# A two-layer vision tower on one core: layer 1 runs twelve attention tiles ahead of layer 2 instead of eight

## The reference, cut to what matters

```python
h = patches(x) @ W.T                                   # 3136 tokens x 192
h = layernorm(h + attn1(h))                            # 12 heads of 16, 49 tokens each
# layer 2
probs   = softmax(h @ Wg.T + bg); top_w, top_idx = top_k(probs, 2)
hw      = (h @ A + ba) * combine[:, :, None]           # 8 experts x rank 16
qkv     = h @ Wqkv.T + bqkv + 2 * (hw @ Bm + combine @ bb)
h = layernorm(h + softmax(q k^T / 4) v @ Wproj.T + bproj)
```

## Time and profile before

| | |
|---|---|
| median of 3 runs | 392.89 us (392.25 to 393.26) |
| the profiled execution, its time | 392.47 us |
| its span, first to last instruction | 390.7 us |
| mean granted clock of TensorE | 0.998 |
| busy: TensorE matmuls, weight loads, VectorE, ScalarE, GpSimd | 373.3, 327.3, 301.5, 218.5, 124.6 us |
| first transpose of probabilities (start of slot 1), of tile 63 (end of slot 63) | 24.58 us, 380.93 us |

### The profile page before, as it was taken

The page is one execution under the profiler, slowest core; times in us unless marked ns, Lnnn a source line. Parts: engine busy times, 40 slices in busy tenths (PEclk is TensorE's granted clock), DMA queues, the critical chain, the costliest instruction groups (busy, mean ns, idle before and its releaser), DMA issues.

```text
span 390.7 us, 13738 instructions
## 1 busy us (share of the span) xinstructions
PE 373.3 (96%) x5312; PEld 327.3 (84%) x5312; DVE 301.5 (77%) x814; ACT 218.5 (56%) x692; POOL 124.6 (32%) x262
## 2 busy tenths in 40 slices
PE   5999999999999999999999999999999999989984
PEld 4888788988888898988889889888888978878973
DVE  7367777687777788987878888787798888698872
ACT  1344646564646645566655566655664565664642
POOL 1312422321433424133315233341325241423313
PEclk9999999999999999999999999999999999999999
DMA  8732522121131122210123201111011101110111
GB/s 269 232 99 62 137 55 54 36 55 48 20 110 24 26 39 73 81 59 9 18 66 70 66 8 29 17 31 22 21 17 29 29 21 19 18 33 14 25 36 37
DMA packets 49338, 20.68 MB, mean 53 GB/s; under 512 B 41262, under 2 KB 45713, under 8 KB 49274
## 3 DMA queue, kind: packets, MB, share of 16 engines
q1 hardware_dynamic: 45530, 10.43, 12.7%
q10 hardware_dynamic: 3744, 9.38, 7.6%
HBM read 12.57 MB, written 2.41 MB: 38 GB/s over the span
## 4 chain that ended last, share of the span: by engine, by line
PE 86%; DVE 5%; ACT 3%; issue 2%; DMA 2%; POOL 1%; SPq 0%; POOLq 0%; ACTq 0%
PE ps L494 12%; PE ps L572 9%; PE ps L599 9%; PE ps L610 7%; PE ps L584 6%; PE ps L621 5%; PE ps L544 4%; PE ps L548 4%; PE ps L546 4%; PE ps L622 4%; PE ps L524 3%; PE ps L530 2%; PE ps L528 2%; PE ps L566 2%; PE ps L642 2%; PE ps L632 2%
## 5 line engine op out<-in xcount | busy, mean ns | idle before, releaser
L965 DVE TENSOR_REDUCE psum<-probs 113x12 f32<-113x588 f32 x64 | 48.6, 760 | 33.9 <-ACT probs L808 33.9
L822 ACT COPY pt<-ps 113x339 f32<-113x339 f32 x128 | 50.2, 445 | 33.4 <-PE ps L599 32.8
L939 DVE TENSOR_REDUCE mx<-ps 113x12 f32<-113x588 f32 x64 | 48.7, 761 | 17.1 <-PE ps L572 16.6
L494 PE MATMUL ps<-tokw,xs 128*128 128x192 f32 (+1 forms) x300 | 56.3, 336 | 4.4 <-DMA tokw<-in_tokw 4.1
L443 POOL TENSOR_SCALAR shift<-mv,rstd 128x1 f32<-128x1 f32 (+1 forms) x50 | 14.2, 283 | 141.6 <-ACT rstd L857 141.6
L432 POOL TENSOR_SCALAR kbd<-k,const 64x294 f32<-64x294 f32 x64 | 34.7, 552 | 73.2 <-ACT q L801 67.5
L494 PEld LDWEIGHTS ps<-tokw,xs 128*128 128x128 f32 (+1 forms) x300 | 48.9, 192 | 7.1 <-DMA xs<-in_x 4.7
L599 PE MATMUL ps<-const,probs 113*113 113x113 f32 x384 | 50.0, 266 | 4.6 <-DVE probs L974 4.0
L599 PEld LDWEIGHTS ps<-const,probs 113*113 113x113 f32 x384 | 44.3, 178 | 9.5 <-issue 8.0
L974 DVE TENSOR_TENSOR probs<-probs,rsum 113x588 f32<-113x588 f32 x64 | 50.1, 782 | 2.2
L946 DVE TENSOR_TENSOR probs<-ps,mx 113x588 f32<-113x588 f32 x64 | 49.4, 772 | 2.2
(11 more groups left out here) (93 smaller groups left out, 785.0 us busy)
## 6 DMA issues: line engine op xcount, KB each, us to landing
xs<-in_x ACTq DMA_DIRECT2D x22, 384.0 KB, 3.8
vbd<-vrow SPq DMA_DIRECT2D x160, 18.4 KB
out<-o SPq DMA_DIRECT2D x24, 96.0 KB, 1.8
xs<-in_x SPq DMA_DIRECT2D x2, 384.0 KB, 6.4
tokw<-in_tokw ACTq DMA_DIRECT2D x3, 192.0 KB, 3.6
w<-in_w SPq DMA_DIRECT2D x1, 472.5 KB, 4.2
xs<-in_x SPq DMA_DIRECT2D x3, 128.0 KB, 3.4
add<-in_add SPq DMA_DIRECT2D x1, 361.5 KB, 7.2
```

The source lines that it names most:

```text
L494: last = nc.tensor.matmul(ps[0:k, bank, 0:E], xs[:, b % XS, m, 0:k], tokw[:, m, :], start=(m == 0), stop=(m == KX - 1))
L822: nc.scalar.copy(pt[n % 2][:, 3 * half:3 * half + 3, :].rearrange("p g i -> p (g i)"), ps[0:PP, 2 + half, 0:3 * PP]).then_inc(pt_ready[hal ...
L939: nc.vector.tensor_reduce(mx[n % 2][:].rearrange("p (b h) -> p b h", b=2), score_view(n), AX.X, ALU.max).then_inc(mx_ready, 1)
L965: nc.vector.tensor_reduce(psum[:].rearrange("p (b h) -> p b h", b=2), probs_view(n), AX.X, ALU.add).then_inc(sum_ready, 1)
```

## The change

`LEAD` goes from 8 to 12, and the planner's slots follow from it. Worked through with 12, the arithmetic gives the plan below. "qk+v 22" is `project_qk2` and `project_v` of block 22, "L1 9" `project_qkv1` of block 9, "emb" an embedding, "t1" `transpose_h1` and `route`, "hw" `transpose_hw`, "out" an output projection counted in the slot by the timing above.

| slot | before | after |
|---|---|---|
| 6 | t1 2, qk+v 0, hw, out | t1 2, emb 8, hw, out |
| 7 | L1 7, emb 8, hw, out | L1 7, emb 9, hw, out |
| 8 | t1 3, qk+v 1, out | t1 3, L1 8, out |
| 9 | t1 4, emb 9, hw | t1 4, L1 9, emb 10, hw |
| 10 | t1 5, qk+v 2, hw | t1 5, qk+v 0, hw, out |
| 13 | L1 9, out | t1 7, L1 11, emb 12, hw |
| 25 | emb 16 | L1 15, out |
| 26 | t1 11, qk+v 8, hw, out | L1 16, emb 17, hw, out |
| 52 | t1 21, qk+v 18, hw | t1 22, out |
| 53 | L1 24, out | qk+v 18, hw, out |
| 54 | qk+v 19, hw, out | t1 23, qk+v 19, out |
| 55 | qk+v 20, out | t1 24, qk+v 20, hw, out |
| 56 | t1 22, out | qk+v 21, hw, out |
| 57 | qk+v 21, hw, out | qk+v 22, out |
| 58 | t1 23, out | qk+v 23 |
| 59 | t1 24, qk+v 22 (urgent), hw, out | out |
| 60 | qk+v 23, hw, out | qk 24 (urgent), out |
| 61 | qk+v 24 (urgent) | nothing but its tile |
| 62 | out | v 24, out |
| 63 | out | out |

Slots with only a layer 1 projection and no output projection are 17, 43 and 51 before, 47 after. Slots with only an embedding are 25 and 33 before, 21, 29 and 37 after. Slots in which `transpose_h1` uses bank 6 are 4 and 5 before, 4, 5, 8, 9 and 13 after. The slots of the after plan that are neither in the table nor named here repeat kinds of the before plan, up to a `transpose_h` more.

Three more edits go with it. The values of the last block are projected in slot 62, after the scores of tile 63, into bank 7, and `keep_busy` and the scores of tile 63 wait accordingly. `inverse_deviation` of layer 1 goes ahead of `take_y` in a slot n when slot n+1 has a `transpose_h1` and no output projection (with a norm to do in slots 9, 13, 21, 29, 37, 47 and 53 of the after plan). `h1_bank` gets a branch for bank 5 in slots with an urgent block; the only such slot of the after plan is 60, which has no `transpose_h1`, so the branch is never taken.

```diff
--- before.py
+++ after.py
@@ -29,7 +29,7 @@
 HB2 = 8
 AW = NB + S - 1
 RING = 6 * T
-LEAD = 8
+LEAD = 12
 XS = 5
 OS = 3
 VR = 6
@@ -152,6 +152,8 @@
 
 def h1_bank(n):
 
+    if any(urgent(b) for b in qkv2s(n)):
+        return 5
     return 6 if turns(n) and not qkv2s(n) else 4
 
 
@@ -555,7 +557,7 @@
                     if n == LAST:
 
                         pe.wait_ge(L2.qk_ready, BLOCKS)
-                        pe.wait_ge(L2.v_rows, BLOCKS)
+                        pe.wait_ge(L2.v_rows, BLOCKS - 1)
                     else:
                         pe.wait_ge(sub_ready, n)
                 else:
@@ -576,12 +578,12 @@
                                 start=(L is L2), stop=(L is L2 or m == 2))
                 last.then_inc(scores_done, 1)
 
-            def project_v(L, b, parts, free):
+            def project_v(L, b, parts, free, bank=5):
                 k = tokens(b)
                 if free:
                     pe.wait_ge(*free)
                 for m, (src, w) in enumerate(parts):
-                    last = nc.tensor.matmul(ps[0:k, 5, 0:E], src[:, 0:k], w[:, V0:V0 + E],
+                    last = nc.tensor.matmul(ps[0:k, bank, 0:E], src[:, 0:k], w[:, V0:V0 + E],
                                             start=(m == 0), stop=(m == len(parts) - 1))
                 last.then_inc(L.v_done, 1)
                 return L.v_rows, b + 1
@@ -658,7 +660,7 @@
 
             def keep_busy(count):
 
-                pe.wait_ge(hw_ready, BLOCKS)
+                pe.wait_ge(L2.v_rows, BLOCKS)
                 for _ in range(count):
                     nc.tensor.matmul(ps[:, 7, 0:128], ident, ident, start=True, stop=True)
 
@@ -701,9 +703,13 @@
                         keep_busy(3)
                     if n == LAST - 1:
                         scores(L2, attention(LAST)[1], LAST)
+
+                        project_v(L2, BLOCKS - 1, values2(BLOCKS - 1), (hw_ready, BLOCKS), 7)
                 for b in turns1(n):
                     if h1_bank(n) == 6:
                         bank6 = transpose_h1(b, 6, bank6)
+                    elif h1_bank(n) == 5:
+                        bank5 = transpose_h1(b, 5, bank5)
                     else:
                         bank4 = transpose_h1(b, 4, bank4)
                 for b in qkv2s(n):
@@ -713,7 +719,8 @@
                         pe.wait_ge(b2_loaded, 16)
                     if urgent(b):
                         bank4 = project_qk2(b, bank4)
-                    bank5 = project_v(L2, b, values2(b), bank5)
+                    if b < BLOCKS - 1:
+                        bank5 = project_v(L2, b, values2(b), bank5)
                     if not urgent(b):
                         bank4 = project_qk2(b, bank4)
                 for b in turns(n):
@@ -807,12 +814,12 @@
                 p = probs[n % 2][:, :, 0:S]
                 nc.scalar.activation(p, p, ACT.Exp).then_inc(exp_ready, 1)
 
-            def take_v(L, b, at, slot_of):
+            def take_v(L, b, at, slot_of, bank=5):
                 k = tokens(b)
                 act.wait_ge(L.v_done, b + 1)
                 if b >= VR:
                     act.wait_ge(pv_done, slot_of[last_tile(b - VR)] + 1)
-                nc.scalar.copy(L.vrow[b % VR][0:k], ps[0:k, 5, at:at + E]).then_inc(L.v_rows, 1)
+                nc.scalar.copy(L.vrow[b % VR][0:k], ps[0:k, bank, at:at + E]).then_inc(L.v_rows, 1)
 
             def take_pt(n):
                 if n >= 2:
@@ -883,13 +890,20 @@
                     take_k2(b)
                     if turns(n) or embeds(n) or urgent(b):
                         take_q2(b)
-                    if urgent(b):
+                    if urgent(b) and b < BLOCKS - 1:
                         take_v(L2, b, 0, SLOT2)
                 for b in turns(n):
                     take_v(L1, b, NB, SLOT1)
                 if not (n <= 1 and turns(n)):
                     for b in embeds(n):
                         take_h(b, embed_bank(n))
+                if n == LAST - 1:
+                    take_v(L2, BLOCKS - 1, 0, SLOT2, 7)
+
+                norm_first = bool(turns1(n + 1) and not out1(n + 1) and not out2(n + 1))
+                if norm_first:
+                    for b in out1(n):
+                        inverse_deviation(L1, b)
                 if before:
                     take_y(n - 1, u)
                 if n == LAST - 1:
@@ -899,8 +913,9 @@
                     for b in qkv2s(n):
                         if not urgent(b):
                             take_q2(b)
-                for b in out1(n):
-                    inverse_deviation(L1, b)
+                if not norm_first:
+                    for b in out1(n):
+                        inverse_deviation(L1, b)
                 for b in routers(n):
                     take_hw(b)
 
```

## The result

The changed kernel takes 400.76 us (median of 4 executions, 396.51 to 404.53) against 392.57 us of the kernel before beside it (392.11 to 393.26, 4 executions): ratio 1.0165, 95% interval 1.0123 to 1.0207. That is slower, as forecast, but outside the forecast's range of 392.3 to 397.0 us.

A forecast was written before the change was run, and what follows sets the result against it. The prediction took TensorE's own stream, busy 373.3 of 390.7 us at full clock, to bound the kernel. Losses of 6.65 us less gains of 4.8 us gave +1.9 us, a median of 394.8 us, range 392.3 to 397.0 us.

The forecast's parts named there:

- the clock rival: Half-empty slots 59 and 61 halve TensorE's clock, doubling slot 60's packed work: about +6, so 401 us; chance 0.03.
- the sum: Whole schedule: losses 6.65 us less gains 4.8 us, net +1.9 us, median 394.8 us; chance 0.60.
- Slot 59 at 4.5 us: Tile and one output projection, late scores: 4.5 us for packed 2.4, lost 2.0 us.
- Slot 61 at 4.5: Tile alone, maximum pushed back by slot 60's statistics: 4.5 us for packed 1.73, lost 2.6 us.
- Slot 62, forecast at 5.4: Last block's values hidden in slot 62, but slot 61's statistics delay its first maximum: lost 0.3 us.
- Bank 6 in slots 8, 9 and 13: `transpose_h1` there waits for the same slot's residual: lost 0.3, 1.0 and 1.0, together 2.3 us.
- Slots 22, 30 and 38: Earlier inverse deviation covers the wait for the normalised block: 7.0 and not 7.5 us, gained 0.9 us.
- Slot 25: Layer 1 projections in a row make `transpose_h` wait for bank 5: 0.45 us added, slot at 5.0 us.
- The late values: `project_v` of the last block leaves slot 60, 1.0 us less; its transfers stay hidden before tile 63's weighing.
- No change: Rival: empty slots close at 3.96 us and half the residual loss is gone: 392.6 us; chance 0.20.
- faster: Rival: the end runs at VectorE's pace, slots 59 and 61 at 3.1 us each: 391.4 us; chance 0.10.
- Late values: Rival: last values copied 2 us later, tile 63's weighing waits for its DMA: +1.5 us, 396.3 us; chance 0.07.

The follow-up runs named there:

- the filled kernel: Changed kernel with matmuls on the identity, result unread, in slots 59 (three and five) and 61 (three and seven): 394.80 us, ratio 1.0047.
- the kernel with slot 59 filled: Changed kernel with eight matmuls on the identity, result unread, in slot 59 alone: 398.26 us, ratio 1.0115.
- both filled a little: Changed kernel with only three matmuls on the identity, result unread, at the beginning of each of slots 59 and 61: 397.29 us, ratio 1.0097.
- slot 61 filled: Changed kernel with 3 and 7 matmuls on the identity, result unread, in slot 61 alone: 400.05 us.

## Why the prediction was wrong

**The step that failed is the clock rival.** It named the mechanism, the place (slot 59 or 61, both half empty), the consequence (slot 60 at half speed, parts of 61 and 62 no longer hidden) and the price, +6 us. It was then given 0.03 and left outside the range, and the sum priced a fall of the clock at nothing, where it measured 7.8 us. Two arguments were used against it. "TensorE still works in each of these slots" is what the changed kernel refutes: 3.02 us of work in 4.47, with no gap above 0.71 us, lowered the clock. "The clock stays up over slot 62's 1.13 us of idle time" rested on a slot that `keep_busy` fills, and the run without it shows the fall. The prediction also named 3.54 of 4.28 us the least busy window of the earlier trace rows; by its share that is slot 62, the filled one (3.96 of 5.09). The trace of before had no unprotected slot as empty as 59, so it could not speak against the rival. The text said so itself ("which no stretch of this trace shows after the start"), and that should have made an open question of it, not an improbable one.

The Trainium skill ("TensorE: Matmul & The Clock Gate", Part 1) was cited for the rule that the clock is halved after long idleness. The same part of the Trainium skill, in its section "A second HAM failure mode", tells of a kernel whose short idle times between groups of matmuls let the clock go back and forth. That passage speaks for the rival, and the runs here agree with it (gaps of at most 0.71 us in slot 59); it was not weighed.

**The size.** By the slots of the filled kernel the fall costs 3.05 us in slot 60, 4.07 in 62 and 0.16 in 63. Slot 61 takes 3.96 us unfilled at full clock (the kernel with slot 59 filled), so it costs 0.48 there. That is 7.8 us for a forecast of 6. Taken from 401.84 it leaves 394.1, where the sum had said 394.4. In the medians filling recovers 6.0 us (400.76 to 394.80), with its own cost in it.

**The sum at full clock, by its terms.**
- Slots 1 to 59 take 340.1 us after and 336.4 before, +3.6. Slots 60 to 63 took 19.9 before; at full clock they would be 4.55, 3.96, 4.97 and 4.12, together 17.6, which is -2.3. Net +1.3, against the +1.9 of the sum. The ratio of the filled kernel, 1.0047, is +1.8 us with the 0.8 us that filling costs in slots 59 and 61 (5.06 for 4.47, 4.17 for 3.96), which leaves 1.0. Less the same 0.8 us, the medians (394.80 against 392.35 us) give 1.7 and the slots of the filled kernel 1.5. So the schedule by itself loses 1.0 to 1.7 us.
- Slot 59 at 4.5 us: 4.47. Slot 61 at 4.5: its 4.44 is the time behind a slow slot 60; at full clock it is 3.96, as slot 25, and the term was 0.5 us too high. Slot 62, forecast at 5.4, is 4.97 in the filled kernel, no longer than the 5.08 of before; slot 60, forecast at 4.8, is 4.55.
- Bank 6 in slots 8, 9 and 13: five waits in place of two, as said. Slots 5 and 9 are equal at 7.96 us, slot 8 is 5.84, slot 4 5.97. The waits rose by 1.3 us (0.8 to 2.1), where the sum had 2.3; no run shows whether the other 1.0 us is lost.
- Slots 22, 30 and 38: 7.14, 7.14 and 6.97 us for an expected 7.0. Without the early `inverse_deviation` they are 7.47 or 7.48 (the runs with only `LEAD`), so the mechanism is shown; in slots 22 and 30 it gains 0.34 of the 0.47. The list of its places had one wrong: slot 5 is one and slot 53 is not, since an output projection follows it (the copy of the weighed values is at 329.08 there, the inverse deviation at 329.74). It changes nothing, as slot 5 takes 7.96 us in both kernels.
- Slot 25, for which the forecast was 5.0 us, takes 4.83 us. In the chain of waits the first `transpose_h` of block 16, whose weight load waits for `take_qk1`, advances by 0.32 us at 176.71 where the one of the slot before advances by 0.11 at 171.94. So bank 5 costs about 0.2 us and not 0.45.
- The late values: the last weighing, at 391.57, waits for no DMA. Slot 60 is 1.1 us shorter without them (5.67 against 4.55), for a forecast of 1.0.
- The rest: by the forecast's own terms slots 60 to 63 would be 1.1 us shorter than before (4.8, 4.5, 5.4 and 4.12, against 19.9), which leaves +3.0 for slots 1 to 59. Measured are +3.6. Slots 22, 30 and 38 account for 0.25 of this; slot 55, at 6.93 us the longest of the slots from 51 to 58, was not priced by itself. No run takes this part further.

**The rivals.** No change and faster: both need two cheaper empty slots (3.96 or 3.1 us each). Slot 59 at 4.47 us speaks against both; slot 61 at 3.96, and waits for the residual that rose by less than priced, speak for part of the first. Late values did not occur. The bank 5 branch is never taken, as stated; with `LEAD` at 8 it is.

**The whole change.** `LEAD` at 12 alone loses 10 us, and filling gives 5.3 of them back (402.62 to 397.28). The other two edits win: 1.5 us of the medians with `LEAD` at 8 (392.35 to 390.83), and with filling 2.5 at 12 (2.1 by the slots). What stays open: what sets apart the executions that escape the fall, and what decides how long the low clock lasts.

## What to carry to other kernels

When a schedule is moved, list its emptiest slots and ask what each does to TensorE's clock, not only what idle time it adds: here two half-empty slots cost 7.8 us, nearly all of it in their full neighbours. A row that seems to show the clock surviving idle time proves it only if nothing in the kernel was put there to hold it, so look for such fillers first. A few matmuls that nobody reads, placed in the idle time of such a slot, can hold the clock: with three in each the clock still fell in eight of ten executions, with eight and ten it held in all ten.

## What the runs showed of the hardware that was not expected

- The clock fell with TensorE busy for 3.02 of 4.47 us and idle for at most 0.71 us in one piece. It held over slot 58 of before with 3.54 of 4.28 busy, and over slot 62 of before with 3.96 of 5.09, all of whose idle time lies in one piece of 1.13 us. So the longest single gap did not tell which slot lowers the clock.
- The fall does not come at once, nor at a fixed distance: mostly 0.4 to 1.6 us into the slot behind the half-empty one (1.05 in the changed kernel, at 365.9; 0.83 without `keep_busy`, at 378.0; 1.55 with both filled a little, at 376.7), but with slot 61 filled 0.6 us before slot 59 ends (364.8).
- Full work does not bring the clock back soon. It stayed at 1.2 GHz for 20.5 us in the changed kernel, 20.5 with only `LEAD` at 12, 17.1 with slot 61 filled, 6.8 with slot 59 filled, and 3.4 with both filled a little. With slot 61 filled TensorE had no idle time for 16.25 us of it.
- The same program can fall or not: two of twelve executions escaped with slot 61 filled, two of ten with both filled a little, one of six with slot 59 filled. The changed kernel itself fell in all four (mean clock 0.970 to 0.990), by different amounts: they span 396.5 to 404.5 us, where those of the kernel before beside it span 1.2 us.
